# Item tiles issued in front of the Gram stores, and three stores issued from ScalarE's queue

## The chip, the core and the metric

The kernel runs on one core of a Trainium2 chip. The core has TensorE (PE in the profile), VectorE (DVE), ScalarE (ACT), GpSimd (POOL) and SyncE (SP). Each works through its own instructions in order, and they meet only at semaphores. A transfer is issued as an instruction of SP, ACT or POOL and is carried by the core's 16 DMA engines. The metric is the time of one execution in microseconds (us).

## The reference

It is one layer of a language model over 8 sequences of 512 tokens with 256 channels: an embedding, an attention-like layer and a mixture of experts. Cut to what matters:

```
h = embeddings[x]
a = layernorm(h)
k, q, v = short_conv(a @ W.T + bias, conv)          # 4 taps, for each of k, q, v
beta = sigmoid(a @ Wbeta.T + bbeta)
k, q = k / |k|, q / |q|;  v = silu(v)               # 16 heads of 16
# chunks of tokens, W the state carried from chunk to chunk:
T   = tril(beta * k @ k.T, -1)
U   = inv(I + T) @ (beta * v - beta * k @ W)
W   = W + k.T @ U                                   # and a weighted mean of W
O   = q @ W_avg * a + q @ W * c + (T_mat * (q @ k.T)) @ U
h = h + rmsnorm(O) @ Wout.T + bout
h = h + experts(layernorm(h))                       # 2 of 8 experts a token, and a shared one
```

## The kernel before

The kernel works in three stages. The **first stage** goes over the 8 batches (sequences). The **second** goes through the recurrence over chunks of 32 tokens, in 32 steps, four sequences side by side. The **third** is the experts.

One batch `b` of the first stage goes as follows. TensorE turns the normalized input and makes six projections `project(b, 0..5)` (line 569), ScalarE evicts each of them twice, as `cv` (line 693) and `raw` (line 696), and VectorE adds the three other taps of the convolution (`tap`, line 794), which read `raw`. Norms, v, k and q follow. Then `gram(b, half)` (line 615) computes the Gram matrices and scores in two halves, which VectorE evicts as `ng` (line 866) and `sT` (line 871). `beta(b)` (line 559) uses the same PSUM tile and therefore waits for the last `sT` eviction of batch b-1. Between its other work VectorE inverts the Gram matrices of batch b-1 and b-2 in half steps (`half_step`, lines 172 and 175). Their input `nx` is loaded by SP from the stored Gram matrices of the batch (line 493), and their output is stored by `store_inverse` (line 184) one batch later.

With the inverse of a batch at hand, its four tiles of 128 tokens are **items**: item `r` of batch `r // 4` is worked on three batches later (`AHEAD = 3`), four items a batch, in the gaps of the projections. An item needs its inverse tiles `xbd` and the beta-k/v tile `bv_i` (`load_x`, line 218), then its scores `sbd` and queries `q_i` (`load_scores`, line 231). TensorE does `apply_inverse` (line 290), `turn_yz`, `apply_scores` (line 312) and `turn_syz`; ScalarE follows with `solved_out`, `turned_out`, `scored_out` and `inner_out`; `store_y` and `store_rest` (lines 242 and 248) store the results, z and inner in four transfers of 32 tokens and the queries in one. GpSimd sums the queries (lines 273 and 278). Items 0 to 19 run in batches 3 to 7, items 20 to 31 in the recurrence steps.

All of these transfers are issued by SP in the fixed order written in `sync` (line 446). In a batch from 3 on (with r = 4(b - 3), so that items r to r+3 are worked on) it is: `move_item` of items r and r+1, `store_inverse(b-2)`, `move_item(r+2)`, 16 stores of q, 4 of k, 2 of Gram, one of beta-k/v, `move_item(r+3)`, 2 of Gram, the `nx` load, the scores store. `move_item(r)` loads x of item r+1, stores y of item r, stores the rest of item r-1 and loads the scores of item r+1. So x of the first item of the next batch is loaded by `move_item(r+3)`, and x of its second item by the first `move_item` of the next batch. A wait in this order holds up everything behind it. On TensorE `apply_inverse` of item 0 stands between `project(b, 0)` and `project(b, 1)`, that of item 1 between `project(b, 2)` and `project(b, 3)`.

The buffers `kk`, `bv`, `ng` and `sT` lie in the space of `h`. The next batch's writes wait for the stores, and at the start of the second stage GpSimd clears `h` once they have landed (lines 1024 and 1030).

Of the kernel before, what the change touches and what calls it, by code (L numbers as in the profile page):

```python
# [105 lines left out]
def build(nc, ids, ids_lane, emb, wqkv, wbeta, wout, router, conv_w, qkv_b, bbeta, bout, rms, const, w_in, w_sw, w_out, out,  # L106
# [14 lines left out]
    with ExitStack() as top:  # L121
# [126 lines left out]
        def store_rest(sp, r):  # L248
            b, t, i = r // TILES, r % TILES, r % 2
            sp.wait_ge(T["z_ready"], r + 1)  # L250
            sp.wait_ge(T["inner_ready"], r + 1)
            for c in range(CH):
                sp.dma_start(zo_dram[t * CH + c, b], zo_out[i][tok(c)].rearrange("p w h d -> p (w h d)")
                             ).then_inc(s_zo_st[i], 16)
# [80 lines left out]
        def turned_out(act, r, bank):  # L335
            act.wait_ge(T["yz_turned"], r + 1)
            if r:
                act.wait_ge(T["scored"], r)
            act.copy(yz_tok[:].rearrange("p h x -> p (h x)"), bank[:]).then_inc(T["yz_ready"], 1)
            if r >= 2:  # L340
                act.wait_ge(s_zo_st[r % 2], 16 * CH * (r // 2))
            act.copy(zo_out[r % 2][:, 0], bank[:].rearrange("p (h w d) -> p h w d", w=2, d=DH)[:, :, 1, :]).then_inc(T["z_ready"], 1)
# [16 lines left out]
        def first_stage(ctx):  # L359
# [86 lines left out]
            def sync(sp, start_next):  # L446
# [11 lines left out]
                for b in range(B):  # L458
                    r = TILES * (b - AHEAD)
                    if b >= AHEAD:  # L460
                        move_item(sp, r)
                        move_item(sp, r + 1)
# [11 lines left out]
                    sp.wait_ge(s_kt, b * 2 + 2)  # L474
                    sp.wait_ge(s_ktri, b * TILES + TILES)
                    for c in range(CH):
                        sp.dma_start(kk_dram[:, b].rearrange("(t c) i x -> c i t x", c=CH)[c],
                                     kk[tok(c)].rearrange("p t h w d -> p t (h w d)")).then_inc(s_kst, 16)
                    for half in range(2):
# [6 lines left out]
                        if half == 0:  # L486
                            sp.wait_ge(s_bv, b * 4 + 4)
                            sp.dma_start(bv_dram[b].rearrange("(t p) x -> p t x", p=P),
                                         bv[:].rearrange("p t h w d -> p t (h w d)")).then_inc(s_st, 16)
                            if b >= AHEAD:  # L490
                                move_item(sp, r + 3)
# [3 lines left out]
                    sp.wait_ge(s_sT, b * TILES + TILES)  # L495
                    sp.dma_start(sT_dram[b].rearrange("(t p) x -> p t x", p=P),
                                 sT[:].rearrange("p t g x -> p t (g x)")).then_inc(s_st, 16)
                    if b == AHEAD - 1:
                        load_x(sp, 0)
                        load_scores(sp, 0)  # L500
# [171 lines left out]
            def scalar(act):  # L672
# [8 lines left out]

                act.wait_ge(s_w, 16 * 7)
                act.wait_ge(s_now, 1)
                root_of_variance(0)
                for b in range(B):
# [4 lines left out]
                    item(b - 1, 3, inner_out, 1)  # L690
                    for n in range(6):
# [192 lines left out]
        def second_stage(ctx):  # L884
# [83 lines left out]
            def load_step(sp, s):  # L968
# [5 lines left out]
                if c % CH == 0:  # L974
                    sp.wait_ge(s_y_st[t % 2], 16 * done)
                    sp.wait_ge(s_zo_st[t % 2], 16 * CH * done)
# [801 lines left out]
```

## Time and profile before

| | us |
|---|---|
| median of 3 runs | 1499.64 (1498.28 to 1503.63) |
| the profiled execution | 1499.78 |
| its span, first to last instruction | 1498.0 |
| TensorE matmuls busy | 1181.4 (79%) |
| VectorE busy | 762.3 (51%) |
| ScalarE busy | 516.6 (34%) |
| GpSimd busy | 390.3 (26%) |
| first stage | 0 to about 576 |
| recurrence steps | about 574 to 898 |
| experts | about 898 to the end |

The busy times are averages over three stages with different limits, so they don't say what bounds the stage that is changed. Issuing a transfer isn't counted as busy; the profile shows it on the queue of the issuing engine (SPq, ACTq). The mean granted TensorE clock was 0.877 of full speed.

### The profile page before, as it was taken

To read this page: it belongs to the slowest core of one execution; us is meant where nothing else is said; L and a number is where in the kernel's file an instruction comes from. 1 tells how busy PE (TensorE), PEld (TensorE's weight loads), DVE (VectorE), ACT (ScalarE), POOL (GpSimd) and SP (SyncE) were. 2 spreads that over 40 slices of the span, in tenths; PEclk is the share of its full clock that TensorE was granted. 3 is DMA by queue.
4 is the path that set the end of the run, shared out by engine and by line. 5 is a ranking of instruction groups with operands and counts; after the bars stand their busy time and mean duration, and the time that the engine had idled before them with its cause. 6 is when DMAs were issued, how large, how long until landed. Compare 5 with 4: busy or idle time off the path is not lost. (4 is left out here: it accounts for less than half of the span.)

```text
span 1498.0 us, 28824 instructions
## 1 busy us (share of the span) xinstructions
PE 1181.4 (79%) x10846; PEld 795.5 (53%) x10846; DVE 762.3 (51%) x1707; ACT 516.6 (34%) x1049; POOL 390.3 (26%) x366
## 2 busy tenths in 40 slices
PE   4855465666666564787688988999999999999997
PEld 2643344353535352566466764665566666666664
DVE  4699959586868685478547873122111121111111
ACT  3454245453636261234152323331122222222221
POOL 6100123131112021533136004661022222222222
PEclk9878778787888785578788988999999999999999
DMA  7754557768695869688687748952122232323222
GB/s 265 195 125 125 129 165 171 225 149 245 136 255 120 253 134 267 200 244 246 172 256 230 222 129 338 346 167 78 28 47 47 45 48 43 47 47 46 47 46 30
DMA packets 237366, 228.68 MB, mean 153 GB/s; under 512 B 88980, under 2 KB 177972, under 8 KB 236080
## 3 DMA queue, kind: packets, MB, share of 16 engines
q1 hardware_dynamic: 202944, 194.28, 45.8%
q0 software_dynamic: 16368, 19.96, 7.7%
q10 hardware_dynamic: 17920, 12.59, 2.8%
q8 instruction: 91, 1.49, 0.4%
q14 instruction: 43, 0.35, 0.1%
HBM read 117.39 MB, written 115.62 MB: 156 GB/s over the span
## 5 line engine op out<-in xcount | busy, mean ns | idle before, releaser
L1683 DVE TENSOR_TENSOR hid_all<-p_s,silu 128x512 f32<-128x512 f32 x103 | 71.2, 691 | 379.4 <-PE p_s L1534 249.7
L1733 POOL DMA_INDIRECT out_h<-y_sb,x_in x71 | 110.5, 1557 | 360.9 <-DVE y_sb L1695 338.4
L1591 ACT ACTIVATE silu<-p_m 128x512 f32<-128x512 f32 x103 | 61.6, 598 | 328.0 <-PE p_m L1527 223.3
L801 DVE SCALAR_TENSOR_TENSOR cv<-raw,conv_sb,cv 128x512 f32<-128x512 f32 x144 | 116.5, 814 | 84.6 <-ACT raw L696 83.6
L172 DVE TENSOR_TENSOR prod<-nx,xt 128x62 f32<-128x62 f32 (+15 forms) x248 | 139.3, 562 | 2.5
L175 DVE TENSOR_TENSOR xt<-xt,prod 128x62 f32<-128x62 f32 (+15 forms) x248 | 138.4, 558 | 4.3
L290 PE MATMUL p_item<-xbd,bv_i 128*32 128x128 f32 x1024 | 48.1, 347 | 110.5 <-DMA xbd<-chunk_inverse_dram 37.6
L1549 PE MATMUL p_y<-wo,hid_all 128*128 x568 | 134.4, 379 | 0.8 <-ACT hid_all L1608 0.8
L1527 PE MATMUL p_m<-wi,xT_c 128*128 x284 | 133.6, 592 | 0.5 <-ACT xT_c L1604 0.5
L1534 PE MATMUL p_s<-ws,xT_c 128*128 x284 | 133.6, 593 | 0.0
L574 PE MATMUL p_p<-xT,wqkv_sb 128*128 128x512 f32 x192 | 108.7, 706 | 0.7 <-ACT xT L688 0.7
L1549 PEld LDWEIGHTS p_y<-wo,hid_all 128*128 128x128 f32 x568 | 102.5, 190 | 12.4 <-issue 1.4
L278 POOL TENSOR_TENSOR qy_out<-qy_out,sy_out 128x512 f32<-128x512 f32 x32 | 46.3, 1448 | 209.7 <-ACT sy_out L351 209.5
L290 PEld LDWEIGHTS p_item<-xbd,bv_i 128*32 128x32 f32 x1024 | 36.6, 138 | 118.8 <-issue 74.1
L273 POOL TENSOR_TENSOR qy_out<-q_i,cst_early 128x512 f32<-128x512 f32 x32 | 39.4, 1232 | 227.8 <-DMA q_i<-q_channels_dram 227.7
L628 PE MATMUL p_g<-kqM,kT 32*32 32x128 f32 x2048 | 50.5, 350 | 51.1 <-DVE h L871 34.5
L1723 POOL DMA_INDIRECT slots_in_dram<-rows,slot_of x64 | 62.1, 971 | 46.7 <-ACT rows L1599 33.1
L1527 PEld LDWEIGHTS p_m<-wi,xT_c 128*128 128x128 f32 x284 | 53.9, 190 | 38.4 <-issue 34.8
L1695 DVE COPY y_sb<-p_y 128x256 f32<-128x256 f32 x71 | 30.2, 425 | 85.6 <-PE p_y L1549 85.6
L628 PEld LDWEIGHTS p_g<-kqM,kT 32*32 32x32 f32 x2048 | 42.5, 126 | 58.0 <-issue 54.6
L693 ACT ACTIVATE cv<-p_p,now_b,conv_sb 128x512 f32<-128x512 f32 x48 | 37.5, 781 | 85.8 <-PE p_p L574 85.6
L1534 PEld LDWEIGHTS p_s<-ws,xT_c 128*128 128x128 f32 x284 | 48.5, 190 | 34.4 <-issue 34.4
(155 smaller groups left out, 2124.4 us busy)
## 6 DMA issues: line engine op xcount, KB each, us to landing
slots_in_dram<-xt SPq DMA_DIRECT2D x18, 520.0 KB, 5.5
x_in<-slots_in_dram SPq DMA_DIRECT2D x71, 130.0 KB, 2.1
q_channels_dram<-qT SPq DMA_DIRECT2D x128, 64.0 KB
k_tokens_dram<-h SPq DMA_DIRECT2D x32, 256.0 KB
chunk_gram_dram<-h SPq DMA_DIRECT2D x32, 256.0 KB, 4.4
beta_kv_dram<-h SPq DMA_DIRECT2D x8, 1024.0 KB
nx<-chunk_gram_dram SPq DMA_DIRECT2D x8, 1024.0 KB, 6.3
scores_dram<-h SPq DMA_DIRECT2D x8, 1024.0 KB
```

What stands on the lines that cost most here:

```text
L172: ins = dve.tensor_tensor(pr, nx[b % 2][:, m, :, 0:m].rearrange("p e k -> p k e").unsqueeze(3).to_broadcast([P, m, 2, w]), xt[b % 2][:, m, ...
L175: ins = dve.tensor_tensor(kept, kept, pr, ALU.add)
L290: ins = pe.matmul(bank[C * f:C * f + C, n * P:(n + 1) * P], bv_i[r % 2][:, 4 * n + f, :], xbd[:, :, 4 * n + f, :], start=True, stop=True)
L574: ins = pe.matmul(p_p[n % 2][:], wqkv_sb[:, k, p, m * P:(m + 1) * P], xT[:, k, :], start=(k == 0), stop=(k == KH - 1))
L628: ins = pe.matmul(p_g[c * C:(c + 1) * C, g % 4, t % 2, g // 4, :], kT[r, g // 4, tok], kqM[r, g // 4, :, :, tok].rearrange("p w e i -> p ( ...
L801: ins = dve.scalar_tensor_tensor(cv[:, p, m, :], raw[:, p, m, j:j + L], conv_sb[:, p, m, j:j + 1], cv[:, p, m, :], ALU.mult, ALU.add)
L1527: ins = pe.matmul(p_m[n % 2][:], xT[s % 2][:, k, :], wi[:, e, k, :], start=(k == 0), stop=(k == KH - 1))
L1534: ins = pe.matmul(p_s[n % 2][:], xT[s % 2][:, k, :], ws[:, e, k, :], start=(k == 0), stop=(k == KH - 1))
L1549: ins = pe.matmul(p_y[s % 2][:, 0, :], hidT[s % 2][:, f * P:(f + 1) * P], wo[:, e, f, :], start=(f == 0), stop=(f == FK - 1))
L1683: dve.tensor_tensor(dst, p_s[n % 2][:], silu[n % 2][:], ALU.mult).then_inc(S["hid_ready"], 1)
L1723: pool.indirect_dma_start(xs_dram, bass.IndirectOffsetOnAxis(slot_of[:, t, k:k + 1], 0), rows[q][:, k, :], None).then_inc(s_scat[q], 16)
L1733: pool.indirect_dma_start(token_rows, bass.IndirectOffsetOnAxis(x_in[s % X_IN][:, D:D + 1].bitcast(U32), 0), y_sb[s % 2][:], None, compute ...
```

## The change

- x and beta-k/v tiles, results and scores of the items move in SP's order. In a batch from 3 on, x of item r+4 (the first of the next batch) is loaded, y of item r+3 and the rest of item r+2 are stored right after the 16 stores of q, in front of the Gram stores; its scores are loaded between the two Gram halves. Behind the second half, and in front of the `nx` load, x of item r+5 is loaded and y of item r+4 stored. The first item's x and scores (`load_x(0)`, `load_scores(0)`) are loaded in front of batch 2's Gram stores. The next batch begins with the rest of item r-1 and the scores of item r+1.
- Scores, beta-k/v and k are stored by ScalarE. k: after `solved_out` of item 3 of the batch. beta-k/v: in the next batch, in front of the first projection's evictions. Scores: in the next batch, after the second projection's evictions and `scored_out` of item 0. Those of the last batch follow its last item.
- z and inner of an item are stored by one transfer of 128 tokens, no longer by four, and the counts that wait for it change from 16 * CH to 16.

The second stage's own order of loads is as it was. The diff, cut:

```diff
@@ store_rest @@
-            for c in range(CH):
-                sp.dma_start(zo_dram[t * CH + c, b], zo_out[i][tok(c)]...).then_inc(s_zo_st[i], 16)
+            sp.dma_start(zo_dram[t * CH:(t + 1) * CH, b], zo_out[i][:]...).then_inc(s_zo_st[i], 16)
@@ sync, for b in range(B) @@
                     if b >= AHEAD:
-                        move_item(sp, r)
+                        if r:
+                            store_rest(sp, r - 1)
+                        load_scores(sp, r + 1)
                         move_item(sp, r + 1)
                     if b >= 2:
                         store_inverse(sp, b - 2)
...
-                    sp.wait_ge(s_kt, b * 2 + 2)
-                    sp.wait_ge(s_ktri, b * TILES + TILES)
-                    for c in range(CH):
-                        sp.dma_start(kk_dram..., kk[tok(c)]...).then_inc(s_kst, 16)
+                    if b == AHEAD - 1:
+                        load_x(sp, 0)
+                        load_scores(sp, 0)
+                    if b >= AHEAD:
+                        load_x(sp, r + 4)
+                        store_y(sp, r + 3)
+                        store_rest(sp, r + 2)
                     for half in range(2):
                         sp.wait_ge(s_ng, b * TILES + 2 * half + 2)
...
-                        if half == 0:
-                            sp.wait_ge(s_bv, b * 4 + 4)
-                            sp.dma_start(bv_dram[b]..., bv[:]...).then_inc(s_st, 16)
-                            if b >= AHEAD:
-                                move_item(sp, r + 3)
+                        if half == 0 and b >= AHEAD:
+                            load_scores(sp, r + 4)
+                    if AHEAD - 1 <= b < B - 1:
+                        load_x(sp, r + 5)
+                        store_y(sp, r + 4)
                     sp.wait_ge(s_ngst, 64 * (b + 1))
                     sp.dma_start(nx[b % 2][:]..., n_dram[b]...).then_inc(s_nx, 16)
-                    sp.wait_ge(s_sT, b * TILES + TILES)
-                    sp.dma_start(sT_dram[b]..., sT[:]...).then_inc(s_st, 16)
-                    if b == AHEAD - 1:
-                        load_x(sp, 0)
-                        load_scores(sp, 0)
@@ scalar @@
+                def store_beta_kv(b):
+                    act.wait_ge(s_bv, b * 4 + 4)
+                    act.dma_start(bv_dram[b]..., bv[:]...).then_inc(s_st, 16)
+
+                def store_scores(b):
+                    act.wait_ge(s_sT, b * TILES + TILES)
+                    act.dma_start(sT_dram[b]..., sT[:]...).then_inc(s_st, 16)
+
+                def store_k(b):
+                    act.wait_ge(s_kt, b * 2 + 2)
+                    act.wait_ge(s_ktri, b * TILES + TILES)
+                    for c in range(CH):
+                        act.dma_start(kk_dram..., kk[tok(c)]...).then_inc(s_kst, 16)
...
                     item(b - 1, 3, inner_out, 1)
+                    if b:
+                        store_beta_kv(b - 1)
                     for n in range(6):
...
                             item(b, 0, scored_out, 0)
+                            if b:
+                                store_scores(b - 1)
...
                     item(b, 3, solved_out, 0)
+                    store_k(b)
                     item(b, 3, turned_out, 1)
                 item(B - 1, 3, scored_out, 0)
                 item(B - 1, 3, inner_out, 1)
+                store_beta_kv(B - 1)
+                store_scores(B - 1)
```

## Rows read from the trace of the kernel before

**Rows 1.** The chain that ended last, by time: start us, us, what.
```profile
898.14 7.12 DMA wo<-in_w_out
```

**Rows 2.** Windows: us, busy PE, PEld, DVE, ACT, POOL; PEclk, DMA share, GB/s.
```profile
423.00:499.00 76.00, 46.24 (x644) 33.58 (x645) 60.00 (x116) 37.61 (x68) 13.56 (x11) 0.81 0.73 187
```

**Rows 3.** Waits of VectorE, 170 to 577 us: total us, times, longest.
```profile
DVE cv L801 <- ACT raw L696: 73.2, 14, 17.0
DVE norm L833 <- ACT norm L720: 6.9, 5, 2.7
```

**Rows 4.** Timeline of VectorE: start us, us, instruction, [idle before <-releaser].
```profile
122.24 0.74 DVE L801 SCALAR_TENSOR_TENSOR cv<-raw,conv_sb,cv 128x512 f32<-128x512 f32 x1
...
130.48 0.75 DVE L801 SCALAR_TENSOR_TENSOR cv<-raw,conv_sb,cv 128x512 f32<-128x512 f32 x1 [1.25 <-ACT raw L696]
...
145.51 0.22 DVE L172 TENSOR_TENSOR prod<-nx,xt 128x62 f32<-128x62 f32 x1
...
182.49 0.74 DVE L801 SCALAR_TENSOR_TENSOR cv<-raw,conv_sb,cv 128x512 f32<-128x512 f32 x1
...
499.32 0.74 DVE L801 SCALAR_TENSOR_TENSOR cv<-raw,conv_sb,cv 128x512 f32<-128x512 f32 x1
...
523.51 0.75 DVE L801 SCALAR_TENSOR_TENSOR cv<-raw,conv_sb,cv 128x512 f32<-128x512 f32 x1 [9.27 <-ACT raw L696]
...
575.13 0.68 DVE L871 TENSOR_TENSOR h<-p_g,cst_early 128x512 f32<-128x512 f32 x1
```

**Rows 5.** Timeline of TensorE in the batches.
```profile
121.94 3.57 PE L565 MATMUL p_g<-wbeta_sb,xT 128*128 128x16 f32 x16 [7.46 <-DVE h L871]
...
483.44 3.30 PE L628 MATMUL p_g<-kqM,kT 32*32 32x128 f32 x128 [4.25 <-DVE h L871]
...
498.98 1.93 PE L290 MATMUL p_item<-xbd,bv_i 128*32 128x128 f32 x32 [9.67 <-issue]
...
516.98 1.94 PE L290 MATMUL p_item<-xbd,bv_i 128*32 128x128 f32 x32 [6.95 <-DMA xbd<-chunk_inverse_dram]
```

**Rows 6.** Timeline of the SP queue: batch 6's end, batch 7's start.
```profile
473.83 11.12 SPq L471 DMA_DIRECT2D q_channels_dram<-qT  x16
485.05 3.01 SPq L477 DMA_DIRECT2D k_tokens_dram<-h  x4
488.10 2.67 SPq L482 DMA_DIRECT2D chunk_gram_dram<-h  x2
490.81 1.71 SPq L488 DMA_DIRECT2D beta_kv_dram<-h  x1
492.64 3.13 SPq L227 DMA_DIRECT2D xbd<-chunk_inverse_dram  x4
...
496.81 1.89 SPq L253 DMA_DIRECT2D z_and_inner_dram<-zo_out  x4
...
506.19 0.34 SPq L493 DMA_DIRECT2D nx<-chunk_gram_dram  x1
506.57 0.45 SPq L496 DMA_DIRECT2D scores_dram<-h  x1
507.13 2.07 SPq L227 DMA_DIRECT2D xbd<-chunk_inverse_dram  x4
```

**Rows 7.** Waits of the SP queue, 423 to 499 us: us, times, longest.
```profile
SPq L184 <- DVE xt L175: 6.1, 1, 6.1
```

**Rows 8.** Timeline of TensorE and the SP queue in the first recurrence steps.
```profile
583.51 1.93 PE L290 MATMUL p_item<-xbd,bv_i 128*32 128x128 f32 x32 [8.32 <-DMA xbd<-chunk_inverse_dram]
...
600.68 1.94 PE L290 MATMUL p_item<-xbd,bv_i 128*32 128x128 f32 x32 [4.80 <-DMA bv_i<-beta_kv_dram]
...
622.10 7.94 SPq L184 DMA_DIRECT2D chunk_inverse_dram<-xt  x8
...
636.21 1.94 PE L290 MATMUL p_item<-xbd,bv_i 128*32 128x128 f32 x32 [5.85 <-DMA bv_i<-beta_kv_dram]
```

**Rows 9.** Line 1205, issues from ScalarE's queue: ns min/median/max, first and last start.
```profile
L1205 ACTq DMA_DIRECT2D ffn_input_channels_dram<-xnT x32: 520/522/1369, 647.9 to 894.1; - x32
```

More of the change, by code:

```diff
@@ L251, in store_rest @@
             sp.wait_ge(T["inner_ready"], r + 1)
-            for c in range(CH):
-                sp.dma_start(zo_dram[t * CH + c, b], zo_out[i][tok(c)].rearrange("p w h d -> p (w h d)")
-                             ).then_inc(s_zo_st[i], 16)
+            sp.dma_start(zo_dram[t * CH:(t + 1) * CH, b], zo_out[i][:].rearrange("p w h d -> p (w h d)")).then_inc(s_zo_st[i], 16)
             sp.wait_ge(T["q_ready"], r + 1)
@@ L340, in turned_out @@
             if r >= 2:
-                act.wait_ge(s_zo_st[r % 2], 16 * CH * (r // 2))
+                act.wait_ge(s_zo_st[r % 2], 16 * (r // 2))
             act.copy(zo_out[r % 2][:, 0], bank[:].rearrange("p (h w d) -> p h w d", w=2, d=DH)[:, :, 1, :]).then_inc(T["z_ready"], 1)
@@ L473, in sync @@
                                              ).then_inc(s_st, 16)
-                    sp.wait_ge(s_kt, b * 2 + 2)
-                    sp.wait_ge(s_ktri, b * TILES + TILES)
-                    for c in range(CH):
-                        sp.dma_start(kk_dram[:, b].rearrange("(t c) i x -> c i t x", c=CH)[c],
-                                     kk[tok(c)].rearrange("p t h w d -> p t (h w d)")).then_inc(s_kst, 16)
+                    if b == AHEAD - 1:
[5 more added lines that the diff above has]
+                        store_rest(sp, r + 2)
                     for half in range(2):
@@ L485, in sync @@
                             start_next(sp)
-                        if half == 0:
-                            sp.wait_ge(s_bv, b * 4 + 4)
-                            sp.dma_start(bv_dram[b].rearrange("(t p) x -> p t x", p=P),
-                                         bv[:].rearrange("p t h w d -> p t (h w d)")).then_inc(s_st, 16)
-                            if b >= AHEAD:
-                                move_item(sp, r + 3)
+                        if half == 0 and b >= AHEAD:
[3 more added lines that the diff above has]
+                        store_y(sp, r + 4)
                     sp.wait_ge(s_ngst, 64 * (b + 1))
@@ L494, in sync @@
                                  n_dram[b].rearrange("g (c i) x -> (g c) (i x)", i=C)).then_inc(s_nx, 16)
-                    sp.wait_ge(s_sT, b * TILES + TILES)
-                    sp.dma_start(sT_dram[b].rearrange("(t p) x -> p t x", p=P),
-                                 sT[:].rearrange("p t g x -> p t (g x)")).then_inc(s_st, 16)
-                    if b == AHEAD - 1:
-                        load_x(sp, 0)
-                        load_scores(sp, 0)
             def gpsimd(pool):
@@ L680, in item @@
                         step(act, TILES * (b - AHEAD) + k, p_i[bank])
+                def store_beta_kv(b):
+                    act.wait_ge(s_bv, b * 4 + 4)
+                    act.dma_start(bv_dram[b].rearrange("(t p) x -> p t x", p=P),
+                                  bv[:].rearrange("p t h w d -> p t (h w d)")).then_inc(s_st, 16)
+                def store_scores(b):
+                    act.wait_ge(s_sT, b * TILES + TILES)
+                    act.dma_start(sT_dram[b].rearrange("(t p) x -> p t x", p=P),
+                                  sT[:].rearrange("p t g x -> p t (g x)")).then_inc(s_st, 16)
+                def store_k(b):
+                    act.wait_ge(s_kt, b * 2 + 2)
+                    act.wait_ge(s_ktri, b * TILES + TILES)
+                    for c in range(CH):
+                        act.dma_start(kk_dram[:, b].rearrange("(t c) i x -> c i t x", c=CH)[c],
+                                      kk[tok(c)].rearrange("p t h w d -> p t (h w d)")).then_inc(s_kst, 16)
                 act.wait_ge(s_w, 16 * 7)
@@ L975, in load_step @@
                     sp.wait_ge(s_y_st[t % 2], 16 * done)
-                    sp.wait_ge(s_zo_st[t % 2], 16 * CH * done)
+                    sp.wait_ge(s_zo_st[t % 2], 16 * done)
                     sp.wait_ge(s_qy_st[t % 2], 16 * done)
```

## The prediction, made before the changed kernel ran

> **What bounds the kernel now.** I read the chain of waits first, then busy time by stretch, the waits of VectorE, and last the timelines of VectorE, TensorE, the SP queue and ScalarE. The chain that ended last reaches back to 898.14 us only [rows 1]: from there TensorE works through the expert stage, which the change doesn't touch. So the question is how much earlier the front part (batches, then recurrence steps) ends.
>
> Among the batches, batch 2 solves on VectorE but has no item. From its first tap (122.24) to batch 3's (182.49) it takes 60.25 us [rows 4]. From there to the last eviction of batch 7 (575.13 + 0.68) pass 393.3 us, 78.7 a batch, though VectorE is busy for only 60.0 in such a one [rows 2, 4]. The difference is mostly one wait: in 170 to 577 us VectorE waits 73.2 us for raw, ScalarE's eviction of the projections, and 6.9 us for the norms [rows 3]. Raw is late because TensorE, in program order, stands in front of an item's inverse tiles: 9.67 us at 498.98 and 6.95 at 516.98 in batch 7 [rows 5], and likewise in batches 3 to 6. And those are late because the SP queue issues them late: x of batch 7's item 0 goes out at 492.64, behind 16 stores of q (11.12 us of issuing), four of k (3.01), two Gram stores (2.67) and the 1 MB beta-k/v store (1.71); x of item 1 goes out at 507.13, behind nx and the scores store, each 1 MB [rows 6]. Item loads and their queue bound this stage; next is VectorE.
>
> **What the change does.** *Item 0.* Its x tiles now follow q's stores directly. k's stores (3.01), the Gram stores (2.67) and beta-k/v (1.71) leave the front, 7.4 us [rows 6]; four-in-one z/inner stores save more: the four take 1.89 [rows 6], a single one I put at a quarter, 0.47 (bounds 0.34, the shortest single issue shown, and 1.89), so 1.4 for each of the items in front. About 9 us in all, so x is issued some 9 us earlier against the 9.67 us wait. What remains doesn't matter, because TensorE's next wait is beta(b), which needs the last sT eviction of VectorE; batch 2 shows it, 7.46 us of waiting at 121.94 [rows 5]. Item 0 must only be in by then. For batch 3 x(0) moves in front of a whole Gram phase, and the longest of VectorE's waits, 17.0 us [rows 3], goes.
>
> *Item 1.* Its load goes right behind the second half's Gram stores, in front of nx; the scores store comes from ScalarE later. Today TensorE starts on it at 516.98, 9.9 us after its issue began [rows 5, 6]. Afterwards the two 1 MB transfers are not in front, and it needs to be in only after beta, scores of item 0 and project 2. This wait goes too.
>
> *What is late next.* In batch 2 beta starts at 121.94, and the tap of projection 2 waits 1.25 us to 130.48 [rows 4, 5]. With items, scores of item 0 (bounds 1.08 and 1.94: the inverse product of the same size, 1.94 at 516.98 [rows 5]; its half as the low end) stands between. 1.25 + 1.94 = 3.2; I take 3.0 a batch, including what is left for projection 3. It includes beta itself at 3.57 us (121.94) [rows 5].
>
> *Moved to ScalarE.* Six issues a batch. k's four cost 3.01 us on SP [rows 6] and stand before item 3's turned_out and the next xT copies. They delay TensorE's scores of item 3, behind which it waits 4.25 us for VectorE anyway (483.44) [rows 5]: hidden by that wait, and up to 3 us a batch if it were gone. Beta-k/v waits for VectorE's products with k (line 812); behind it queue cv and raw of projection 0, which VectorE reads only after its second half of Gram and score evictions, and these come after those products. The scores store waits for sT, which beta has already waited for. An issue from ScalarE in this kernel takes 0.52 us, at worst 1.37 [rows 9], against 0.44 to 1.7 on SP. I take nothing, bounds 0 and 6 x 1.37 = 8.2 us a batch.
>
> *SP after the change.* In 423 to 499 the longest wait of SP is 6.1 us, for VectorE's inverse [rows 7]; I put all its waits at twice that, so it issues for some 64 of 76 us. It loses 3.01 + 1.71 + 0.45 + 4 x 1.4 = 10.8 us of issuing a batch [rows 6], so 53 have to fit into a batch of 66. It takes on one new wait: load_x and store_y of the next batch's item 0 and 1 stand before the nx load, and need item 0 solved. That is so some 9 us before the Gram stores go out, so the nx load comes no later than today's 506.19, and VectorE wants nx only after all taps.
>
> *Sum for the batches.* Removed 73.2. Added back 5 x 3.0 = 15. Norm waits: ScalarE is no longer late with the squares, 6.9 falls to about 2 (batch 2 has none), so 5. Gain 73.2 - 15 + 5 = 63 us: 393.3 becomes 330, 66 a batch, still above the 60 busy. Bounds: 73 + 7 = 80 if nothing comes back; about 25 if item 1 stays late and ScalarE's issues are exposed.
>
> *Recurrence steps.* x of item 20 is in before the stage starts, so the 8.32 us at 583.51 go. Gram stores, nx and x(21) then no longer queue behind it, and the scores store goes out from ScalarE: the 4.80 us at 600.68 go, and POOL's clear of h, which waits for that store, comes earlier. Of the 5.85 at 636.21 I take 1, because the eight inverse stores (7.94 us at 622.10) still stand before that load [rows 8]. Gain 8.3 + 4.8 + 1 = 14, bounds 8 and 21. The later steps shift as they are.
>
> Total 63 + 14 = 77. The profiled execution took 1499.8 us (span 1498.0 and 1.8 around it), and the median of the runs is 1499.6, so no correction: **1499.8 - 77 = 1423 us**.
>
> **A rule against it.** DMA engines were busy for 0.73 of 423 to 499 [rows 2]; that is 55 of 76 us, or 0.84 of a 66 us batch, and x(1) shows what a backlog costs. The Trainium skill (DMA: Bandwidth & Descriptors, "Issuing engines are not separate DMA queues") says that transfers started by different engines run on the same 16 DMA engines, and that a second issuer saves only issuing time, which is usually small beside the transfer. By that rule the ScalarE queue alone would give next to nothing; the row on SP speaks otherwise here (some 64 us of issuing in a batch), but it supports the second case below.
>
> **Rivals.** *DMA engines stay in the way.* The work fits on average, but bursts (Gram stores, x, nx, scores, all within 15 us) keep item 1's tiles late. The waits before the fourth projection, about 39 us (9.27 in batch 7 at 523.51, and one such in each of the batches 4 to 6) [rows 4], stay, and only 34 of 73.2 go; steps give 8. 1499.8 - 42 = 1458. For: share 0.73 already, and x(1)'s 9.9 us. Against: the two 1 MB transfers that stood before it no longer do.
>
> *Nothing is given back.* The taps never wait, as the item products run at the high clock: 80 + 20 = 100, so 1400. Against: batch 2's wait of 1.25 without any item.
>
> *Slower: the nx load behind item 0.* SP may not issue nx(b) until TensorE has solved the next batch's item 0 and ScalarE has written its y. If x(0) lands late, nx is late, and VectorE, which solves in order between its other work, stops where today it doesn't. It starts the solve of a batch some 23 us after the first tap (145.51 against 122.24 in batch 2) [rows 4] and nx needs 6.3 us to land (the page's median), so each microsecond counts once nx goes out over 17 us after the first tap, against 7 today (506.19 against 499.32) [rows 4, 6]. To lose more than is won, it must go out over 17 + 77/5 = 32 us after; at 34 us the batches would lose 5 x 17 = 85 against the 63 won there, and the time be 1499.8 + 22 - 14 = 1508. For: the wait is real and in order. Against: x(0) would have to take over 20 us longer than the 9.9 us that x(1) took behind 2 MB.
>
> *It doesn't do what it says*: SP reaches x(0) no earlier because q's stores already fill the time: within 0.5% of before. Against: 7.4 us of issuing stand after them.
>
> **Chances.** Forecast 0.58; DMA engines 0.25; nothing given back 0.08; slower 0.05; no effect 0.04. Likeliest 1423. The range runs from 1400 to 1462: it holds the forecast's own spread (1405 to 1445) and most of the DMA case. A measurement of this kernel can tell 0.5% (7.5 us) from nothing. Faster 0.91, same 0.04, slower 0.05.
>
> **What would show it.** Right: waits of VectorE for raw fall from 73 to about 15 us, each at the third projection; TensorE's waits on x tiles between batches are gone, and its wait for beta on VectorE takes their place; SP waits for VectorE's inverse and second Gram half grow; batches last 66 us; ScalarE's waits don't end in its own issues. Wrong: waits of VectorE before the fourth projection stay at 9 us (DMA case), VectorE waits for nx (slower case), or ScalarE's issues take over 1 us each and taps wait for them.

## The result and the profile after

The changed kernel takes 1486.12 us (median, 1483.15 to 1488.08), beside 1501.44 for the kernel before, run with it: a ratio of 0.9896, 95% interval 0.987 to 0.9922. It is faster by 1.0%, some 15 us. Forecast were 77 us. The profiled execution has a span of 1483.3 us and a mean granted clock of 0.887 (before 0.877).

The chain that ended last still begins where the experts do (start us, us, what), now at 883.22 and not at 898.14 [rows 1]:

```profile
883.22 6.72 DMA wo<-in_w_out
```

So the 15 us were won in front of the experts. Two windows split them: from batch 3's first tap to batch 7's last eviction, and one batch (us, busy PE, PEld, DVE, ACT, POOL; PEclk, DMA share, GB/s).

```profile
182.48:554.77 372.29, 239.48 (x3307) 171.90 (x3306) 303.31 (x558) 182.88 (x329) 77.04 (x64) 0.81 0.73 195
...
404.36:483.56 79.20, 51.44 (x682) 36.63 (x681) 61.55 (x116) 38.79 (x70) 13.47 (x11) 0.83 0.72 190
```

The five batches went from 393.3 to 372.3 us, 21 less, and the recurrence steps from 322.3 (575.8 to 898.1) to 328.5 (554.8 to 883.2), 6 more. That is the 15. From first tap to first tap (batch 7: to its last eviction) batches 3 to 7 took 81.8, 80.7, 78.4, 75.9 and 76.5 us and take 67.3, 77.3, 77.3, 79.2 and 71.2. Batch 3 alone gives 14.5 of the 21: its first item no longer waits, where it waited longest (before, then after). Batch 6 is longer than it was.

```profile
196.96 1.94 PE L290 MATMUL p_item<-xbd,bv_i 128*32 128x128 f32 x32 [25.01 <-DMA bv_i<-beta_kv_dram]
190.62 1.08 PE L288 MATMUL p_item<-xbd,bv_i 128*32 128x128 f32 x32
```

The waits of VectorE in that stretch (us, times, longest) answer to [rows 3]:

```profile
DVE cv L820 <- ACT raw L710: 43.1, 15, 7.1
DVE norm L852 <- ACT norm L736: 10.9, 5, 2.9
```

Waits for raw fell by 30.1 us, norm waits rose by 4.0, waits for p_g of the turned norms fell by 1.7, and VectorE's busy time rose from 296.6 to 303.3 for the same 558 instructions, 6.7: 30.1 - 4.0 + 1.7 - 6.7 = 21.1, the whole gain of the batches. The 6.7 go with where GpSimd's instructions fall. A tap beside one of them can take 1.59 us, one without 0.74:

```profile
198.05 1.90 POOL L271 TENSOR_TENSOR qy_out<-q_i,cst_early 128x512 f32<-128x512 f32 x1 [7.58 <-DMA q_i<-q_channels_dram]
198.91 1.59 DVE L820 SCALAR_TENSOR_TENSOR cv<-raw,conv_sb,cv 128x512 f32<-128x512 f32 x1
201.75 0.74 DVE L820 SCALAR_TENSOR_TENSOR cv<-raw,conv_sb,cv 128x512 f32<-128x512 f32 x1
```

Against the shortest of the same line and shape, VectorE's instructions that overlap one of GpSimd's are longer by 21.6 us in all before and by 28.5 after, the others by 1.7 and 2.9. It is the half steps of the inverse that lose more (169.2 us busy before, 182.3 after), while the taps lose less (76.7 and 69.6). Two taps of batch 6 (VectorE's timeline) show that both long waits are still there, shorter, where batch 7 had 9.27 for the fourth projection alone [rows 4]:

```profile
404.36 0.74 DVE L820 SCALAR_TENSOR_TENSOR cv<-raw,conv_sb,cv 128x512 f32<-128x512 f32 x1
...
413.74 0.75 DVE L820 SCALAR_TENSOR_TENSOR cv<-raw,conv_sb,cv 128x512 f32<-128x512 f32 x1 [2.38 <-ACT raw L710]
...
424.05 0.75 DVE L820 SCALAR_TENSOR_TENSOR cv<-raw,conv_sb,cv 128x512 f32<-128x512 f32 x1 [7.10 <-ACT raw L710]
```

TensorE's timeline says why. Items still wait for their inverse tiles, and now for their scores too, which none of [rows 5] shows:

```profile
400.67 1.94 PE L288 MATMUL p_item<-xbd,bv_i 128*32 128x128 f32 x32 [7.44 <-DMA xbd<-chunk_inverse_dram]
...
417.85 1.93 PE L288 MATMUL p_item<-xbd,bv_i 128*32 128x128 f32 x32 [5.10 <-DMA xbd<-chunk_inverse_dram]
428.31 1.87 PE L310 MATMUL p_item<-sbd,yz_tok 128*32 128x128 f32 x32 [3.53 <-DMA sbd<-scores_dram]
```

The sum of its waits for scores in that stretch is new, 20.6 us:

```profile
PE p_item L310 <- DMA sbd<-scores_dram: 20.6, 9, 3.7
```

The SP queue, at the border of batches 5 and 6, answers to [rows 6]:

```profile
376.96 16.71 SPq L471 DMA_DIRECT2D q_channels_dram<-qT  x16
393.80 1.90 SPq L227 DMA_DIRECT2D xbd<-chunk_inverse_dram  x4
...
399.80 3.66 SPq L484 DMA_DIRECT2D chunk_gram_dram<-h  x2
...
408.24 1.06 SPq L484 DMA_DIRECT2D chunk_gram_dram<-h  x2
409.41 4.76 SPq L227 DMA_DIRECT2D xbd<-chunk_inverse_dram  x4
...
415.16 0.78 SPq L494 DMA_DIRECT2D nx<-chunk_gram_dram  x1
416.04 0.56 SPq L252 DMA_DIRECT2D z_and_inner_dram<-zo_out  x1
416.65 0.56 SPq L254 DMA_DIRECT2D queries_dram<-qy_out  x1
417.25 3.85 SPq L236 DMA_DIRECT2D sbd<-scores_dram  x4
```

The order is the intended one, but the issues have grown: q's sixteen take 16.71 us (11.12 in [rows 6]), the four inverse loads of item 1 take 4.76 (2.07), and the four scores loads behind the single z/inner store 3.85. From batch 6's first tap to batch 7's SP issues 82 transfers in 67.9 us, where before it issued 96 in 61.4. Fewer issues took longer. The queries store, issued right behind the z/inner store, shows it from the landing side (last number, median us from issue to landing): 2.9 us before and 8.1 after.

```profile
queries_dram<-qy_out SPq DMA_DIRECT2D x32, 256.0 KB, 8.1
```

### The profile page after: what moved, and what is told of

Its sections match the earlier page's. It is cut to its first block and busy times, and to the rows that moved or that the text cites. A ratio compares the mean times of both kernels' runs of the same rounds, so it can differ in the third digit from the quotient of the medians.

```text
span 1483.3 us, 28728 instructions
## 1 busy us (share of the span) xinstructions
PE 1182.9 (80%) x10846; PEld 795.2 (54%) x10846; DVE 767.8 (52%) x1707; ACT 516.2 (35%) x1049; POOL 391.3 (26%) x366
## 3 DMA queue, kind: packets, MB, share of 16 engines
q1 hardware_dynamic: 187968, 169.10, 40.6%
## 5 line engine op out<-in xcount | busy, mean ns | idle before, releaser
L175 DVE TENSOR_TENSOR xt<-xt,prod 128x62 f32<-128x62 f32 (+15 forms) x248 | 146.5, 591 | 4.3
L172 DVE TENSOR_TENSOR prod<-nx,xt 128x62 f32<-128x62 f32 (+15 forms) x248 | 142.5, 574 | 2.5
L820 DVE SCALAR_TENSOR_TENSOR cv<-raw,conv_sb,cv 128x512 f32<-128x512 f32 x144 | 109.4, 764 | 54.1 <-ACT raw L710 53.1
L569 PE MATMUL p_p<-xT,wqkv_sb 128*128 128x512 f32 x192 | 114.2, 737 | 0.7 <-ACT xT L700 0.7
L288 PE MATMUL p_item<-xbd,bv_i 128*32 128x128 f32 x1024 | 44.4, 327 | 52.3 <-DMA xbd<-chunk_inverse_dram 21.6
L310 PE MATMUL p_item<-sbd,yz_tok 128*32 128x128 f32 x1024 | 43.8, 324 | 44.6 <-DMA sbd<-scores_dram 24.3
L623 PE MATMUL p_g<-kqM,kT 32*32 32x128 f32 x2048 | 46.1, 336 | 34.0 <-DVE h L890 20.5
L569 PEld LDWEIGHTS p_p<-xT,wqkv_sb 128*128 128x128 f32 x192 | 41.5, 237 | 47.6 <-issue 43.2
```

The costliest lines, as they stand in the source:

```text
L172: ins = dve.tensor_tensor(pr, nx[b % 2][:, m, :, 0:m].rearrange("p e k -> p k e").unsqueeze(3).to_broadcast([P, m, 2, w]), xt[b % 2][:, m, ...
L175: ins = dve.tensor_tensor(kept, kept, pr, ALU.add)
L569: ins = pe.matmul(p_p[n % 2][:], wqkv_sb[:, k, p, m * P:(m + 1) * P], xT[:, k, :], start=(k == 0), stop=(k == KH - 1))
L820: ins = dve.scalar_tensor_tensor(cv[:, p, m, :], raw[:, p, m, j:j + L], conv_sb[:, p, m, j:j + 1], cv[:, p, m, :], ALU.mult, ALU.add)
```

## The experiments

The change has three parts that can be switched apart: the order of the item tiles (O), one z/inner store in place of four (M), and three stores from ScalarE (S). Of the seven mixes beside the kernel before six were run. Every ratio is to the kernel before on the same chip.

| kernel | ratio | interval |
|---|---|---|
| S | 0.9859 | 0.9835 to 0.9882 |
| M | 1.014 | 1.0097 to 1.0182 |
| O | 0.9912 | 0.9878 to 0.9946 |
| O + M | 1.0077 | 1.005 to 1.0103 |
| O + S | 0.976 | 0.9721 to 0.98 |
| O + M + S (the change) | 0.9896 | 0.987 to 0.9922 |

**O + M**, the changed kernel with the three stores back on SP:

```diff
-                    store_k(b)                 # scalar; and beta-k/v, scores
+                    for c in range(CH):        # sync, in front of the Gram stores
+                        sp.dma_start(kk_dram..., kk[tok(c)]...).then_inc(s_kst, 16)
```

> The changed kernel with k, beta-k/v and scores stored by SP again (k in front of the first Gram half, beta-k/v behind it, scores behind the nx load); order of the item tiles and the single z/inner store kept. Theory A (elastic issuing): an issue on SP takes as long as the transfers before it need to drain, so taking six issues to ScalarE freed nothing: SP's issues in one batch (69 to 70 us for 83 of them after, 62 to 65 for 97 to 102 before) stay at 66 to 71 for 89, and the time is that of the changed kernel within 6 us, 1480 to 1492. Rival B (issue time is owned by the instruction, and the move to ScalarE did save its 5 us a batch): 5 batches x 5 us slower, about 1510. Rival C (the move hurt, through ScalarE's stalls of 3.7 us behind the k stores and two queues sharing): 1465 to 1478.

**S**, the kernel before with these three stores taken to ScalarE at the places of the change:

```diff
-                        sp.dma_start(kk_dram..., kk[tok(c)]...).then_inc(s_kst, 16)
+                    store_k(b)                 # scalar; and beta-k/v, scores
```

> The kernel before with only the three stores moved to ScalarE; SP's order of the rest and the four z/inner stores as before. Theory A: within 5 us of before, 1495 to 1504; 16 stores of q and four of k together take 14 us of issuing before, and q's alone take about that now. Rival B: x of item 0 is issued 5 us earlier in batches 3 to 7 and its wait shrinks by that: 1475 to 1482. Rival C: slower than before by 5 to 15 us, since ScalarE stands 3 us behind k's stores and waits for VectorE in front of projection 0's eviction: 1505 to 1515.

**M**, the kernel before with the single z/inner store:

```diff
-            for c in range(CH):
-                sp.dma_start(zo_dram[t * CH + c, b], zo_out[i][tok(c)]...)
+            sp.dma_start(zo_dram[t * CH:(t + 1) * CH, b], zo_out[i][:]...)
```

> The kernel before with only the four z/inner stores of an item made one. My own term for it was 1.4 us of SP issuing an item, 5.6 a batch. Theory A: the next issues take it up, 0 to 5 us faster: 1495 to 1500. Rival B: 5 x 5.6 = 28 us in the batches as long as SP sets the pace, 1470 to 1478.

**x(1) first**, the changed kernel with x of item r+5 and the store of y of item r+4 in front of the second Gram half, and the first loads of the steps in front of batch 7's q stores:

```diff
                     for half in range(2):
+                        if half and AHEAD - 1 <= b < B - 1:
+                            load_x(sp, r + 5)
+                            store_y(sp, r + 4)
                         sp.wait_ge(s_ng, b * TILES + 2 * half + 2)
```

> The changed kernel with two places changed: x of item r+5 and y of item r+4 in front of the second Gram half (not behind it), and the recurrence's first loads in front of batch 7's q stores (not between its Gram halves). If the late x of item 1 comes from standing behind the Gram stores, which take 2.6 to 3 us more of its issue time (4.76 to 5.06 us for four loads, 2.07 before), VectorE's waits before the fourth projection (4 to 7 us a batch) shrink by half, 8 to 12 us in all, and the 21.8 us wait of TensorE for z at the end of batch 7 falls below 10, 8 to 12 us: 1464 to 1472. If SP's total is what binds (theory A), the first part only moves the wait to scores or nx and gives under 4 us, the second still gives its 8 to 12: 1472 to 1478. If neither matters: 1486.

Measured: O + M 1509.78, S 1477.34, M 1520.49, x(1) first 1498.83 us, beside 1501.86 before. The three stores are worth 24 us by the first (1509.8 to the change's 1486.1) and by the second. Theory B, issuing time that SP gets back, had this size right (the reason turned out to be another, below), and S alone does at least as well as the whole change (0.9859 and 0.9896; the intervals just overlap). All theories missed M. It is 19 us slower, by an edit that only takes issues away. In its SP queue the same pattern as in the changed kernel stands alone, the scores loads behind the store at 4.20 us instead of 1.96 in the kernel before (first line):

```profile
499.21 1.96 SPq L236 DMA_DIRECT2D sbd<-scores_dram  x4
...
503.62 0.57 SPq L252 DMA_DIRECT2D z_and_inner_dram<-zo_out  x1
504.24 0.53 SPq L254 DMA_DIRECT2D queries_dram<-qy_out  x1
504.81 4.20 SPq L236 DMA_DIRECT2D sbd<-scores_dram  x4
```

x(1) first made things worse (ratio 0.9975, 0.9946 to 1.0005, against 0.9896), slower than all that was expected of it. The inverse tiles of each batch's second item hardly wait any more (1.5 us in all; those of the first still 19.4), but the second Gram half goes out at 497.73, so that nx follows only at 505.72 and the scores of item 1 at 507.53, and TensorE now stops for these:

```profile
517.12 1.93 PE L310 MATMUL p_item<-sbd,yz_tok 128*32 128x128 f32 x32 [10.95 <-DMA sbd<-scores_dram]
```

The wait of an item moves from one of its tiles to the next one in the queue. It isn't removed: waits for scores among the batches are 48.3 us in all here, 20.6 in the changed kernel.

**What the single z/inner store does.** The packet counts of the profile name a cause (queue, packets, MB, share of 16 engines). SP's queue in the kernel before, and in M:

```profile
q1 hardware_dynamic: 202944, 194.28, 45.8%
```

```profile
q1 hardware_dynamic: 201024, 194.27, 45.8%
```

The difference is 1920 packets at equal data. If each transfer has one packet more for every DMA engine that carries it, 128 stores on 16 engines have 2048, and 32 stores on n engines 32n: 2048 - 32n = 1920 gives n = 4. By that count the 32 single stores run on 4 of 16 engines (no row shows the engines of a single store). The outermost dimension of their DRAM side is the four chunks. The Trainium skill states this rule (DMA: Bandwidth & Descriptors, "Rules for kernel authors", row "Use all 16 engines": an outermost dimension smaller than 16 confines the whole transfer to at most so many engines), and the count agrees with it. Four kernels test it.

**O + S**, the changed kernel with four z/inner stores again:

```diff
-            sp.dma_start(zo_dram[t * CH:(t + 1) * CH, b], zo_out[i][:]...)
+            for c in range(CH):
+                sp.dma_start(zo_dram[t * CH + c, b], zo_out[i][tok(c)]...)
```

> The changed kernel, with the z/inner store split again into four of 32 tokens. Theory D: the single z/inner store does harm because it is carried by 4 of the 16 DMA engines (its DRAM side has an outermost dimension of 4), which lands late itself and fills the queues of these engines in front of the loads behind it; the three parts of the change add up. One z/inner store alone cost 1520.5 - 1501.9 = 18.6 us, so this kernel should take 1486 - 19 = 1467 us (1461 to 1473), the four issues of the sbd scores load behind it should go back from 3.9 us to about 2, and the packets of the SP and ACT queues together should be 1920 more than in the changed kernel. Rival E: with the items issued early and three stores on ScalarE, SP has time to spare, and the form of the z/inner store matters no more or helps: 1480 to 1490 us.

**O + S, first loads early**, the same, and in batch 7:

```diff
+                    if b == B - 1:
+                        start_next(sp)
                     for f in range(4):          # the 16 stores of q
...
-                        if half == 0 and b == B - 1:
-                            start_next(sp)
```

> As the kernel with four z/inner stores again, and in batch 7 the first loads of the recurrence steps are issued in front of the 16 stores of q, instead of behind the first Gram half. Theory: TensorE's wait of 21.8 us for z/inner at 564 us, new in the changed kernel, comes from these loads being issued about 25 us too late; with them in front it goes, and of the 328 us of recurrence steps some 10 to 15 are won: 1467 - 12 = 1455 us. Rival: the first step was not on the path, since the items 20 and 21 bound the start of the steps (8.6 us of wait for bv_i at 611): within 4 us of the kernel with four stores.

**One store, 16 engines**, the changed kernel with the DRAM buffer laid out anew:

```diff
-    zo_dram = ... [NC_BATCH, B, C, 2 * D]
+    zo_dram = ... [B, TILES, P, 2 * D]
-            sp.dma_start(zo_dram[t * CH:(t + 1) * CH, b], zo_out[i][:]...)
+            sp.dma_start(zo_dram[b, t], zo_out[i][:]...)
...
-                sp.dma_start(zo[i][:]..., zo_dram[c, b:b + GROUP]...)
+                for n in range(GROUP):
+                    sp.dma_start(zo[i][n * C:(n + 1) * C]..., zo_dram[b + n, t, c % CH * C:(c % CH + 1) * C])
```

> The changed kernel, still with one z/inner store an item, but the DRAM buffer is laid out by sequence and tile, so that the store writes 128 consecutive rows (no outermost dimension of 4); the recurrence steps then load z/inner in four transfers instead of one (3 more issues on SP in each of 32 steps). Theory D (four engines): the batches run as with four stores or a little better, the stretch from batch 3's first tap to batch 7's last eviction is 352 to 362 us instead of 372, and the scores loads behind the store issue in about 2 us. Rival F (one large transfer is bad whatever carries it, e.g. because a 512 KB store is not interleaved with the loads): the stretch stays at 368 to 376. The steps tell nothing on this, since their loads are changed: time as a whole 1465 to 1490 in either case.

**O**, the kernel before with the changed order alone (four z/inner stores, all stores on SP).

> The kernel before with the changed order of the items in SP's queue alone: four z/inner stores, and the stores of k, beta-k/v and scores on SP (in front of the Gram stores, between its halves and behind nx). Theory D, parts add up: order is worth 1509.8 - 1520.5 = -10.7 us, so 1501.9 - 10.7 = 1491 us (1485 to 1497). Rival: the order helps only in so far as it repairs the late landing of the single z/inner store, and alone it gives nothing: 1498 to 1506. My prediction's first half (item 0's and item 1's waits go by the order alone): 1450 or below.

Measured, beside 1509.39 before on this chip: O + S 1473.72 (0.976), with first loads early 1463.99 (0.9692, 0.9652 to 0.9732), one store on 16 engines 1469.29 (0.9732, 0.9682 to 0.9781), O 1497.98 (0.9912). Splitting the store again takes the change from 0.9896 to 0.976, and one store on 16 engines does as well: the harm isn't in the merging, and as the four stores write the same layout as the single one, it isn't in the layout either. The four engines are what is left, as theory D has it. Its 352 to 362 us for the batches were 358.9 (the rival's store of 512 KB is one of 256), and beside a before of 1501.9 it had 1461 to 1473 for O + S, where 0.976 gives 1466, and 1485 to 1497 for O, where 0.9912 gives 1489; the prediction's own forecast for O, 1450 or below, missed. Its packets confirm the layout; 32 stores on 16 engines and 128 loads instead of 32 make the same sum as O + S, and both have 1920 more than the changed kernel (187968):

```profile
q1 hardware_dynamic: 189888, 169.11, 40.8%
```

VectorE's and TensorE's waits of the 16-engine kernel, 182 to 555 us:

```profile
DVE cv L820 <- ACT raw L710: 25.3, 12, 6.5
...
PE p_g L560 <- DVE h L890: 17.0, 5, 6.8
...
PE p_item L288 <- issue: 14.2, 5, 5.4
PE p_item L310 <- DMA sbd<-scores_dram: 13.6, 5, 4.8
...
PE p_item L288 <- DMA xbd<-chunk_inverse_dram: 6.2, 2, 3.7
```

In the changed kernel raw waits are 43.1 us, and the inverse products (p_item<-xbd) wait 20.5 for their tiles and 12.5 more put down to issue, 33.0; here it is 20.4. Beta waits for VectorE (17.0 us), as the prediction wanted it. In the timeline item 1 of batch 6 waits 0.47 us:

```profile
404.38 3.57 PE L560 MATMUL p_g<-wbeta_sb,xT 128*128 128x16 f32 x16 [3.68 <-DVE h L890]
414.36 1.08 PE L288 MATMUL p_item<-xbd,bv_i 128*32 128x128 f32 x32 [0.47 <-issue]
```

The parts add up. O is worth -0.9% alone, -0.6% beside M, -1.0% beside S; M +1.4, +1.7 and +1.4%; S -1.4, -1.5 and -1.8%. Means of -0.8, +1.5 and -1.6% give -0.9%, and the change measured -1.0%. The profiles say where (us, batches from batch 3's first tap to batch 7's last eviction, steps from there to the experts). There is one of each kernel, and O and O + S are from a chip on which the kernel before takes 1509 us and not 1501, so a few us of a difference may be the chip's.

| kernel | batches | steps |
|---|---|---|
| before | 393.3 | 322.3 |
| S | 376.5 | 310.1 |
| M | 403.7 | 329.0 |
| O | 377.8 | 334.2 |
| O + M | 388.4 | 334.6 |
| O + S | 362.4 | 316.6 |
| O + M + S | 372.3 | 328.5 |

Among the batches O gives 14 to 16 us, S 15 to 17, and M costs 10, whatever stands beside them. In the steps O costs 6 to 12 us and so loses a good part of that again. O alone also shows why it wins so little among the batches: in 170 to 577 us inverse tiles and beta-k/v keep TensorE waiting for only 5.7 us in all (89.7 before), as forecast, but scores wait instead, and ScalarE now waits until the last z/inner of a buffer has landed, which it does neither before nor in S or M:

```profile
PE p_item L312 <- DMA sbd<-scores_dram: 33.8, 8, 7.2
...
ACT zo_out L342 <- DMA z_and_inner_dram<-zo_out: 18.5, 4, 5.9
```

**What ScalarE's queue brings.** Two kernels, both O with four z/inner stores. In the first, k is stored by SP again, beta-k/v and scores by ScalarE. In the second all are on SP, but beta-k/v and scores of batch b-1 are issued in batch b:

```diff
                     r = TILES * (b - AHEAD)
+                    if b:
+                        sp.dma_start(bv_dram[b - 1]..., bv[:]...).then_inc(s_st, 16)
                     if b >= AHEAD:
                         ...
                         move_item(sp, r + 1)
+                    if b:
+                        sp.dma_start(sT_dram[b - 1]..., sT[:]...).then_inc(s_st, 16)
```

> The kernel with the changed order, four z/inner stores and the beta-k/v and scores stores on ScalarE, but the four stores of k back on SP, behind the items and in front of the Gram stores. To compare with the kernel in which all three are on ScalarE (ratio to before 0.976) and with the order alone (0.9912), which differ by 0.0152, 23 us. Theory G: what ScalarE's queue brings is that two 1 MB stores leave SP's burst around the Gram stores and are issued one batch later; k's stores on ScalarE give nothing, since the 16 q stores beside them then issue in 15.0 us instead of 11.2 and ScalarE's next eviction waits 3.7 us behind them: ratio 0.972 to 0.978. Rival H (every microsecond of issuing taken off SP counts, also the 3.3 of k): about half of the 23 us is k's, ratio 0.982 to 0.987.

> The changed order and four z/inner stores, all stores on SP, but beta-k/v and scores of a batch are issued in the next batch, at its start and behind item 1's transfers, about where ScalarE issued them. Theory G (their time of issue matters): ratio 0.974 to 0.980, like the kernel with all three on ScalarE (0.976). Rival H (the queue matters, SP's issuing time): 0.988 to 0.994, like the order alone (0.9912).

Measured, beside 1511.86: 1481.25 (0.9784, 0.9736 to 0.9832) and 1483.78 (0.9815, 0.9759 to 0.987). From O (0.9912) to O + S (0.976) are 0.0152. The later issue of two 1 MB stores alone gives 0.0097 of it, without ScalarE; ScalarE's queue for these two 0.0031 more, and k's four stores 0.0024, both within the intervals. Nearest is theory G, though both kernels lie just above its bands: by the medians most of S is that two megabytes leave the burst around the Gram stores, not that SP is relieved. The k stores show why they bring little. With them on ScalarE q's sixteen stores take 14.96 us of SP in O + S, with them on SP 11.55 in batch 6 of the first kernel here, where k's own take 5.40: most of what leaves SP comes back as slower issues beside it. And ScalarE itself stops behind them, here in the changed kernel:

```profile
461.14 2.83 ACTq L691 DMA_DIRECT2D k_tokens_dram<-h  x2
464.07 0.59 ACT L337 COPY yz_tok<-p_item 128x512 f32<-128x512 f32 x1 [3.72 <-issue]
```

**The candidate.** One store on 16 engines with the first loads early, and the four-store form again:

> Candidate: the changed kernel with the z/inner store of 128 consecutive rows (16 engines) and the first loads of the recurrence steps in front of batch 7's q stores. If what these two gave apart adds up (0.9732 for the first, -0.0068 for the second): ratio to before 0.966, i.e. 1451 us at a before of 1502. Rival: three more loads from SP in each recurrence step eat the gain there, or the early first loads gave nothing and the difference of 10 us was the spread of the runs: 0.971 to 0.975.

> The kernel with four z/inner stores and the first loads of the steps in front, timed again, since its ratio (0.9692, 0.9652 to 0.9732) overlapped with that of the same kernel without the early loads (0.976, 0.9721 to 0.98). Early loads worth 10 us: ratio 0.967 to 0.972. Spread only: 0.973 to 0.979.

Measured, beside 1501.19: 1464.76 (0.9746, 0.9721 to 0.9771) and 1460.63 (0.9718, 0.9692 to 0.9744). The 16-engine form didn't keep its advantage, so between these two nothing is decided by more than their intervals. The best kernel is the changed order, four z/inner stores, three stores on ScalarE and the first loads of the steps in front of the q stores: 2.8% faster than before. The changed kernel's interval (0.987 to 0.9922) lies far from it.

What the early loads give is not settled. Two measurements are 0.9692 and 0.9718, the second inside its band for a gain of 10 us (0.967 to 0.972), without them it is 0.976, and the intervals touch; with the 16-engine store 0.9746 is in the rival's band. By the profiles of the steps they give nothing. The steps by ScalarE's copies of u (step 0, 7 and 31), in the changed kernel:

```profile
565.55 0.37 ACT L1182 COPY u<-p_u_turn_x 128x256 f32<-128x256 f32 x1 [22.66 <-PE p_u_turn_x L1065]
...
662.55 0.37 ACT L1182 COPY u<-p_u_turn_x 128x256 f32<-128x256 f32 x1 [0.65 <-PE p_u_turn_x L1076]
...
867.21 0.37 ACT L1182 COPY u<-p_u_turn_x 128x256 f32<-128x256 f32 x1 [1.79 <-PE p_u_turn_x L1076]
```

in the kernel before:

```profile
575.28 0.37 ACT L1163 COPY u<-p_u_turn_x 128x256 f32<-128x256 f32 x1 [8.82 <-PE p_u_turn_x L1046]
...
683.92 0.37 ACT L1163 COPY u<-p_u_turn_x 128x256 f32<-128x256 f32 x1 [0.64 <-PE p_u_turn_x L1057]
...
880.70 0.37 ACT L1163 COPY u<-p_u_turn_x 128x256 f32<-128x256 f32 x1 [1.78 <-PE p_u_turn_x L1057]
```

and in the last kernel:

```profile
543.49 0.37 ACT L1184 COPY u<-p_u_turn_x 128x256 f32<-128x256 f32 x1 [10.51 <-DVE h L892]
...
646.50 0.37 ACT L1184 COPY u<-p_u_turn_x 128x256 f32<-128x256 f32 x1 [1.90 <-issue]
...
842.84 0.37 ACT L1184 COPY u<-p_u_turn_x 128x256 f32<-128x256 f32 x1 [1.79 <-PE p_u_turn_x L1078]
```

Counted from the end of the batches (before 575.8, after 554.8, last kernel 542.9; in O + S 552.1, with its copies at 556.58, 655.03 and 852.75):

| us | step 0 after the batches | steps 0 to 7 | steps 7 to 31 |
|---|---|---|---|
| before | -0.5 | 108.6 | 196.8 |
| the change | +10.8 | 97.0 | 204.7 |
| O + S | +4.4 | 98.5 | 197.7 |
| O + S, first loads early | +0.6 | 103.0 | 196.3 |

With the loads early step 0 starts 3.8 us sooner than in O + S and the next seven take 4.5 longer (8.0 in the other profile of this kernel): step 0 was not what held the steps. Step 7 comes 102.9 us after the batches in O + S and 103.6 with the loads early.

## Why the prediction was wrong

The direction, and where the waits sit, were right; 77 us were not there. Of the 62 missing, 42 are in the batches (raw waits 28 more than forecast, norms 9, VectorE's own work 6.7, less the 1.7 for p_g) and 20 in the steps. By its steps:

- **The single z/inner store, "a quarter, 0.47", 1.4 us saved for each item.** This step has the largest price of its own. The issue did cost 0.56 us, but the store ran on 4 of 16 engines by its packet count, and what is behind it on these engines waits: shown by M (+19 us), by O + S (1.4% faster than the change) and by the 16-engine form. The transfers' issue times, their landing and their spread over the engines were all taken as unchanged. It accounts for some 22 of the missing 62 us.
- **"x is issued some 9 us earlier".** Before, item 0's x goes out 6.7 us ahead of batch 7's first tap [rows 4, 6]; after, at 471.79 against 483.56, 11.8 ahead: 5.1 earlier. q's stores take 14.97 us there instead of 11.12, which eats 3.85 of the 9. The wait fell from 9.67 to 4.58 (at 476.79) in batch 7 and was still 7.44 in batch 6.
- **"This wait goes too" (item 1).** It fell by half (28.7 us in batches 4 to 7 before, 13.1 after). x(1) is issued right behind the second Gram half, 5.1 us after the tap in batch 6 and 3.9 in batch 7, against 7.8 before, and in the thick of that burst its four loads take 4.76 and 5.06 us to issue (4.99 in O + S, so it isn't the four engines). 8.4 us pass to TensorE's start (9.9 before). That the 1 MB stores no longer stand in front was correct, and the two Gram transfers of the second half stood there in both orders.
- **Nothing said of the scores.** The prediction followed x and stopped. Scores and queries come behind x, and once x is early they are the late ones: 20.6 us of new waits. O alone and x(1) first show it in pure form: x waits of 5.7 us in all beside 33.8 for scores, and a single wait of 10.95. Nor did it ask when a result's buffer comes free: ScalarE waits 10.1 us for z/inner to land in the changed kernel, 18.5 in O.
- **"Added back 5 x 3.0 = 15"** came out as 43.1, and norm waits at 10.9 instead of 2, for all these reasons together. Even in O + S, without the four engines, 26.0 us of raw waits stay.
- **ScalarE's issues at nothing, and SP relieved to 53 us a batch.** SP issues for 67.9 us in batch 6. The four k stores are exposed by up to 3.7 us a batch (15.2 in all before the copies of yz) and slow q's stores; they give nothing measurable. The other two give what S gives, but by their later time. The rule of the Trainium skill that the prediction quoted (DMA: Bandwidth & Descriptors, "Issuing engines are not separate DMA queues"), that a second issuer saves only issuing time, agrees here: of the 0.0152 of S, 0.0097 came without one.
- **Steps: -14 forecast, +6 measured.** The 8.32 us of item 20 did go. The 4.80 and 5.85 of items 21 and 23, put at 0 and 4.85, came out as 5.87 and 8.63, again for the beta-k/v tile. Step 0 starts 11.3 us later, since `start_next` stands behind q's slower stores, x(20) and the Gram stores (TensorE waits 21.8 us for z/inner, 7.95 before), and the next seven take 11.6 less, so that step 7 comes 107.8 us after the batches where it came 108.1 before: nothing is won. Steps 7 to 31 take 7.9 longer (the way from step 31 to the experts gives 1.4 back). What makes these 7.9 isn't shown: single profiles have 0.9 in O + S, 5.4 in O, 2.1 in M and -0.6 in O + M, so neither the order nor the four engines explain them alone.
- **The sum for the DMA case.** The second case put raw waits at 39 us and the time at 1458. 43.1 remained; it named the burst rightly and missed the rest: norm waits, VectorE's 6.7 us and the steps, which it had 8 us shorter.

Open is what lengthens the later steps, how the delay passes from the four engines into SP's issue times (the runs show it by its effect alone), and the mix M + S, which wasn't run.

## What to carry to other kernels

Before merging transfers, look at the slowest dimension of both sides: four transfers of 32 rows over 16 engines beat one of 4 x 32 over four, although three issues are saved, and a rearranged buffer gives both. In a queue that is behind, follow the whole row of loads that the consumer needs, not the first one: moving one forward hands its wait to the next. And price a moved issue by what it does to its neighbours in time; two large stores taken out of a burst, even on the same queue, did most (0.0097 of 0.0152) of what looked like the work of a second queue. Look also at what the engines beside an unchanged one do at the same moment: its work can take longer for that alone.

## What the runs showed that wasn't expected

- A transfer's duration of issue isn't a constant. Four scores loads took 1.96 us before (499.21) and 3.85 to 4.20 behind a store on four engines; sixteen q stores took 10.4 to 13.0 us (mean 11.3) in batches 3 to 7 of the six kernels that store k from SP, and 11.5 to 16.7 (mean 14.8) in the eight in which ScalarE issues k's stores beside them.
- A 256 KB store on four engines moved the landing of the store issued behind it from 2.9 to 8.1 us (8.2 among the batches in M alone), at a DMA share of 0.72 over the batches before and 0.73 after: the average share doesn't see a backlog on four engines.
- nx, issued behind item 1's tiles and not ahead of them, lands among the batches in 8.9 us instead of 6.2 (8.9 in O and in O + S, 6.3 in M, so it is the order and not the four engines), and no wait of VectorE for it shows.
- An order of issue that frees a load can hold a buffer: ScalarE's waits for z/inner to land are 0 before, 18.5 us in O and 35.0 in x(1) first.
